# Attention sums of a macaron block: copied in two pieces, added and normalised on GpSimd into a resident buffer, with an output stage that loads nothing

## The reference

```python
x = x + 0.5 * ffn(layernorm(x), w_gate, w_up, w_down)
x = x + attn(layernorm(x), Wq, Wk, Wv, Wo, We)
x = x + 0.5 * ffn(layernorm(x), w_gate, w_up, w_down)

# attn
ctx = X @ We.T                                   # [1, 4096, 32]
influence = einsum('bqe,bke->bqk', ctx, ctx)
scores = einsum('bhqd,bhkd->bhqk', Q, K) * SCALE + 0.1 * influence[:, None]
out = einsum('bhqk,bhkd->bhqd', softmax(scores), V)
out = out.transpose(0, 2, 1, 3).reshape(b, s, d) @ Wo.T
```

## Time and profile before

| | us |
|---|---|
| median of 3 runs | 4047.24 (4041.54 to 4052.59) |
| the profiled execution | 4050.0 |
| its span | 4048.2 |
| attention's steps, 488 to 3695 | 3207 |
| output stage, 3695 to 3789 | 94 |
| second MLP, 3789 to the end | 259 |

### The profile page before, as it was taken

How to read it: one execution, slowest core, us unless ns; L and a number is a source line. 1 busy time by engine, 2 the same in 40 slices (tenths; PEclk the granted TensorE clock), 3 DMA queues, 4 the chain that set the end, 5 groups by cost and what they waited for, 6 DMA issues and landing times. The chain is left out here.

```text
span 4048.2 us, 91447 instructions
## 1 busy us (share of the span) xinstructions
PE 3807.0 (94%) x29204; PEld 2213.2 (55%) x29204; DVE 3249.4 (80%) x5168; ACT 2490.7 (62%) x2898; POOL 455.4 (11%) x274
## 2 busy tenths in 40 slices
PE   3998599999999999999999999999999999996698
PEld 2986355555555555555555555555555555553598
DVE  6984588878888888788888887888888878885697
ACT  4663266666666666666666666666666666663365
POOL 4980100000000000000000000000000000000397
PEclk7999699999999999999999999999999999997799
DMA  3004412121212121212121212121212121213200
GB/s 123 0 0 148 106 37 44 38 43 37 45 37 44 37 45 40 41 38 46 38 44 37 44 36 45 36 44 36 45 36 44 36 44 36 45 38 78 87 20 21
DMA packets 316697, 186.52 MB, mean 46 GB/s; under 512 B 195488, under 2 KB 246592, under 8 KB 315872
## 3 DMA queue, kind: packets, MB, share of 16 engines
q1 hardware_dynamic: 315248, 181.27, 20.5%
q10 hardware_dynamic: 1136, 1.08, 0.1%
HBM read 147.75 MB, written 33.82 MB: 45 GB/s over the span
## 5 line engine op out<-in xcount | busy, mean ns | idle before, releaser
L1185 DVE TENSOR_REDUCE tops<-coarse 128x1 f32<-128x512 f32 x4144 | 2681.2, 686 | 588.4 <-PE coarse L1046 484.6
L1161 ACT ACTIVATE probs<-fine 128x1024 f32<-128x1024 f32 x2048 | 1998.4, 1021 | 1018.2 <-PE fine L1065 1018.1
L1076 PE MATMUL o_ps<-probs,vh 128*32 128x512 f32 x8192 | 1092.3, 605 | 0.2 <-ACT probs L1161 0.2
L1055 PE MATMUL fine<-query_a,key_a 64*128 64x512 f32 x4096 | 922.7, 447 | 19.8 <-issue 19.1
L1055 PEld LDWEIGHTS fine<-query_a,key_a 64*128 64x128 f32 x4096 | 388.0, 186 | 929.4 <-ACT probs L1161 750.1
L1046 PE MATMUL coarse<-key_a,max_query 64*128 64x512 f32 x4144 | 834.4, 398 | 44.2 <-DMA key_c<-scratch_c_key 23.4
L1065 PE MATMUL fine<-query_b,key_b 33*128 33x512 f32 x4096 | 818.6, 395 | 0.0
L1061 PE MATMUL fine<-query_c,key_c 64*128 64x512 f32 x4096 | 816.3, 394 | 0.0
L1046 PEld LDWEIGHTS coarse<-key_a,max_query 64*128 64x128 f32 x4144 | 395.0, 187 | 114.5 <-DVE tops L1185 29.7
L1065 PEld LDWEIGHTS fine<-query_b,key_b 33*128 33x128 f32 x4096 | 389.2, 186 | 90.3
L1061 PEld LDWEIGHTS fine<-query_c,key_c 64*128 64x128 f32 x4096 | 389.4, 187 | 84.5
(11 more groups left out here) (157 smaller groups left out, 2326.0 us busy)
## 6 DMA issues: line engine op xcount, KB each, us to landing
query_c<-scratch_c_query SPq DMA_DIRECT2D x258, 128.0 KB, 2.7
max_query<-scratch_q_hi SPq DMA_DIRECT2D x524, 32.0 KB, 1.8
max_query<-scratch_c_query SPq DMA_DIRECT2D x262, 64.0 KB, 2.0
query_a<-scratch_q_hi SPq DMA_DIRECT2D x516, 32.0 KB, 1.8
query_a<-scratch_c_query SPq DMA_DIRECT2D x258, 64.0 KB, 2.0
query_b<-neg_max SPq DMA_DIRECT2D x1032, 0.5 KB, 2.0
query_b<-scratch_q_lo SPq DMA_DIRECT2D x258, 32.0 KB, 2.4
scratch_attended<-result SPq DMA_DIRECT2D x512, 8.0 KB
```

The costliest lines, as they stand in the source:

```text
L1055: pe.matmul(fine[i % 2][:, r, :], key_a[kp][half_rows(r, 0, HALF), cols], query_a[half][half_rows(r, 0, HALF), :], start=True, stop=False)
L1076: last = pe.matmul(o_ps[32 * j:32 * (j + 1), :], vh[kp][:, kt, :], probs[:, kt // 2 % RING, kt % 2, :], start=g == 0, stop=g == NG - 1)
L1161: act.activation(probs[:, i % RING, :, :], fine[i % 2][:, :, :], ACT.Exp).then_inc(probs_ready, 1)
L1185: dve.tensor_reduce(tops[n][:, idx // KB, idx % KB:idx % KB + 1], bank[:, :], AX.X, ALU.max).then_inc(tops_ready, 1)
```

## The change

**The sums of a step.** A class `Sums` holds the buffers. ScalarE copies `o_ps` in two pieces of 49 rows into two buffers, both starting at partition 0. GpSimd adds the two (`add_halves`), copies rows 32 to 48 of the sum down to row 0, and adds again (`add_quarters`): `total` has 16 rows of values and one of sums. SyncE copies the row of sums into `few`, 16 partitions of 32 elements; VectorE inverts it behind its eighth coarse reduction (`invert`); SyncE writes it to DRAM and reads it back spread over 16 rows into `wide`; GpSimd multiplies (`multiply`) one step later; and SyncE copies the product into `at`, which stays in SBUF for all 4096 tokens. `finish`, `take_result`, `sel` and the stores of values and sums are gone.

```diff
+    def add_halves(self, eng, s):
+        eng.wait_ge(self.ot_ready, s + 2)
+        eng.tensor_tensor(self.ot[0][:, :], self.ot[0][:, :], self.ot[1][:, :], ALU.add).then_inc(self.half_ready, 1)
+        eng.wait_ge(self.half_ready, s + 1)
+    def add_quarters(self, eng, s):
+        eng.tensor_copy(self.quarter[:, :], self.ot[0][32:32 + self.ROWS, :]).then_inc(self.quarter_ready, 1)
+        eng.wait_ge(self.quarter_ready, s + 1)
+        eng.tensor_tensor(self.total[:, :], self.ot[0][0:self.ROWS, :], self.quarter[:, :], ALU.add).then_inc(self.total_ready, 1)
+    def invert(self, eng, s):
+        eng.wait_ge(self.few_loaded, 16 * (s + 1))
+        eng.reciprocal(self.few[:, :], self.few[:, :]).then_inc(self.inv_ready, 1)
+    def multiply(self, eng, s):
+        eng.wait_ge(self.spread, 16 * (s + 1))
+        eng.tensor_tensor(self.wide[:, :], self.total[0:DK, :], self.wide[:, :], ALU.mult).then_inc(self.result_ready, 1)
...
+                def combine(s):
+                    sums.add_halves(pool, s)
+                    sums.multiply(pool, s - 1)
+                    sums.add_quarters(pool, s)
...
-                    act.wait_ge(fin_ready, F_LEAD + s)
-                    act.activation(ot[:, :], o_ps[:, :], ACT.Copy).then_inc(ot_ready, 1)
+                    act.wait_ge(sums.total_ready, s + 1)
+                    for half in range(2):
+                        last = act.activation(sums.ot[half][:, :], o_ps[2 * 32 * half:2 * 32 * half + 32 + sums.ROWS, :], ACT.Copy)
+                    last.then_inc(sums.ot_ready, 1)
```

```diff
+                def step(s, half, before_last, last):
+                    sp.wait_ge(probs_ready, P_LEAD + PAIRS * s)
+                    if within(s + 1):
+                        load_operand_a(1 - half, query_a, s + 1, q_loaded)
+                    if before_last is not None:
+                        sums.save_inverse(sp, s - 2)
...
+                        load_others(1 - half, s + 1)
+                    if before_last is not None:
+                        sums.spread_inverse(sp, s - 2)
+                        sp.wait_ge(sums.result_ready, s - 1)
+                    if last:
+                        sums.copy_sum(sp, s - 1)
...
+                        sums.store(sp, head, slice(block * QB, (block + 1) * QB) if isinstance(block, int) else bass.ds(block * QB, QB), sums.stored)
+                    if within(s + 1):
+                        load_max(s + 1, 1 - half)
+                    if within(s + 3):
+                        sp.wait_ge(coarse_ready, UNITS // 2 * (s + 2))
+                        load_operand_a(1 - half, max_query, s + 3, mq_loaded)
```

```diff
-                            if unit + 1 == FINISH_AFTER:
-                                before(lambda: finish(s - 1, UNITS * (s + 1) + FINISH_AFTER + 2 - COARSE))
...
+                        place = 2 if i % GROUP != 0 else 1 if unit == SKIP_AFTER + 1 else 0
+                        scores_first(s, half, kp, i)
+                        if place == 0:
+                            maxima(unit)
+                        scores_second(half, i)
+                        if place == 1:
+                            maxima(unit)
+                        scores_last(s, half, kp, i)
+                        if place == 2:
+                            maxima(unit)
```

```diff
+            with eng.Fori(0, H // 2 - 1) as hp:
+                two_heads(hp)
+            two_heads(H // 2 - 1)
...
+                for block in range(NQB - 2):
+                    step((H - 1) * NQB + block + 2, block % 2, (H - 1, block), True)
+                    for dst, src, loaded in reload[block:block + 1]:
+                        sp.dma_start(dst, src).then_inc(loaded, 16)
```

```diff
+                sp.wait_ge(sums.result_ready, LAST)
+                sums.store(sp, H - 1, tokens(NQB - 2), sums.late_stored)
+                for dst, src, loaded in more:
+                    sp.dma_start(dst, src).then_inc(loaded, 16)
+                sums.copy_sum(sp, LAST)
+                sums.save_inverse(sp, LAST)
...
+                def low(b, n):
+                    pool.wait_ge(ahi_ready, b + 1)
+                    if not isinstance(b, int) or b >= 2:
+                        pool.wait_ge(y_ready, b - 1)
+                    pool.tensor_tensor(at_lo[n][:, :, :], at[:, :, tokens(b)], at_hi[n][:, :, :].bitcast(F32), ALU.subtract).then_inc(alo_ready, 1)
```

```diff
+                    if has_next(b):
+                        x_norm(b + 1)
                     for i, (bank, scale, slot) in enumerate(SPLITS):
-                        if i == NEXT_AFTER - 1 and has_next(b):
-                            x_norm(b + 1)
                         if i == NEXT_AFTER and has_next(b):
                             x_lo(b + 1, 1 - n)
```

More of the change, by code:

```diff
@@ new lines, in _ @@
+                step(0, 0, None, False)
+                step(1, 1, None, True)
+                for block in range(2):
+                    step(block + 2, block, (0, block), True)
+                for head in range(H - 1):
+                    with sp.Fori(0 if head else 1, NQB // 2) as i:
+                        for half in range(2):
+                            block = 2 * i + half
+                            step(sp.snap(head * NQB + block + 2), half, (head, block), True)
+                    if head + 2 < H:
+                        load_keys_a(head % 2, head + 2)
+                        load_keys_b(head % 2, head + 2)
@@ new lines, in body @@
+                    if within(s + 2):
+                        reduce_max(s + 2, half, 0)
+                    if within(s + 1):
+                        max_rows(s + 1, 1 - half)
+                    if within(s + 2):
+                        for idx in range(1, INVERT_AFTER + 1):
+                            reduce_max(s + 2, half, idx)
+                    if unless_first is None:
+                        sums.invert(dve, s - 1)
+                    else:
+                        with dve.If(unless_first):
+                            sums.invert(dve, s - 1)
@@ L1359, in macaron_kernel @@
[L1359 to L1364 removed]
+        w_saved, o_reload, ffn_reload = sem("w_saved"), sem("o_reload"), sem("ffn_reload")
```

325 lines of the change are left out of this document (138 added, 187 removed).

## The result

The changed kernel takes **3952.97 us** (median of 4 runs, 3948.77 to 3958.01), the kernel before 4045.8 (4 runs, 4041.54 to 4052.59): a ratio of 0.977, with a 95% interval of 0.9751 to 0.9788. The forecast was 3945 and its range 3925 to 3980. The profiled execution took 3954.89 us, its span 3953.1, so the span is 95.1 us shorter than that of the profiled execution before.

A forecast was written before the change was run, and what follows sets the result against it. TensorE's own instructions were taken as the length of an attention step, VectorE next. Gains of 29 + 5 + 6 + 53 + 9 = 102 us from 4050 gave 3948, less 2.8 to the median 3945 us; range 3925 to 3980.

The forecast's parts named there:

- Part 1: Attention step: `finish` leaves TensorE, saving 0.27 us less a 0.04 wait in each of 127 steps; 29 us, ends 0 and 34.
- Part 2: ScalarE in attention: two copies of the sums instead of one, 598 ns each, nothing on the path.
- Part 3: GpSimd in attention: three two-input operations and a copy, 4.5 to 5.2 us a step, hidden; 0 us.
- Part 4: VectorE's inversion in attention: 0.3 us in idle time, `few` landed at 14.7, due at 18.8; costs nothing.
- Part 5: SyncE's chain ahead of `load_max` in an attention step: ends at 13.2, `load_max` began at 14.1; 0 us, ends 0 and +5.
- The rival with SyncE's chain (4072): Attention: chain DMAs land 2 to 3 us later, `load_max` some 6 late, TensorE waits about 1 us a step; 3%.
- Part 6: Attention's loop over two heads: six jumps back instead of seven, the last heads written out; gain 5 us, ends 0 and 5.5.
- Part 7: Last two attention steps: 24 pairs of coarse tiles beyond the end go, 0.25 us each; 6 us, ends 0 and 9.
- Part 8: Output stage, from attention's last product to the second MLP: 95 us becomes 42.5; gain 53, ends 43 and 55.
- Part 9: Projection: seven of TensorE's eight waits for the normalised block go; gain 9 us, ends 5 and 9.
- the one on the coarse wait: Attention: units 24 and 25 wait in their new place for what `finish` took, part 1 gives 0; 3974 us, 10%.
- GpSimd might block VectorE: Attention: VectorE stands still while GpSimd adds and becomes the bound, a step of 26.65 us; 4215 us, 4%.

The follow-up runs named there:

- experiment 1: The changed kernel with VectorE's reduction of coarse unit 24 reading 256 of its 512 columns: a step of 24.495 us instead of 24.622, a run of 3936.44 us.
- experiment 3: The kernel before without TensorE's adding products (`finish`), units 24 and 25 in the old place, then the new: steps 24.698 and 24.602 us, runs 4043.30 and 4024.10 us.
- Experiment 6: The changed kernel with three, then six more additions of 16x512 on GpSimd in each step: 4128.13 us and 4538.22 us.
- Experiment 5: The kernel before with only the last two heads written out and the projection's block normalised at the head: 4027.76 us, beside 4041.65 us for the kernel before.
- experiment 7: The changed kernel with, by version: all heads written out; all 128 steps, no skipped bank; also two low parts on VectorE: 3930.51, 3910.99, 3909.41 us.
- experiments 1 and 2: The second is the changed kernel with units 24 and 25 in the old place, behind their group's first product pair: a step of 24.710 us, a run of 3967.3.

## Why the prediction was right

**Part 1, `finish`: mis-sized.** Forecast 29 us, measured 16.2 in ordinary steps (0.137 each in place of 0.23). The step that failed is "a wait of 0 to 0.1 is left. I take 0.04". The prediction followed one wait, the one of the moved products (units 24 and 25), and that one costs nothing indeed. It did not follow the consequence of moving the products: their reductions come later by a pair, and the bank of unit 24 is the one that unit 27 wants. That wait takes 0.12 of the 0.26 us between the step before (24.76) and eight plain groups (24.50), where 0.04 were taken; experiment 1, in which it goes, has the step of eight plain groups. What was said of the old place was right: 24.70 to 24.71, nearly everything given back.

**Part 2, ScalarE: right.** 595 ns a copy. That nothing of it is on the path is contained in the 0.02 us of experiment 3.

**Part 3, GpSimd: right.** 1.28 + 1.27 + 0.60 + 1.28 = 4.4 us in a step (4.5 to 5.2 taken). With parts 2 and 5 it costs at most 0.02 us a step, by experiment 3.

**Part 4, the inversion: right** for this kernel. It takes 0.33 us, `few` is issued some 12 us into most steps (15 in the one behind a head's key loads, 11.6 in the one shown below), and VectorE waits for it three times: in the last two steps, where the coarse reductions ahead of it are missing, and in the output stage.

**Part 5, SyncE: the number right, the margin wrong.** `load_max` starts 14.0 us into the step, as reckoned:

```profile
3594.72 0.56 SPq L855 DMA_DIRECT2D few<-total  x1
3595.33 0.59 SPq L870 DMA_DIRECT2D at<-wide  x1
3597.11 5.03 SPq L1037 DMA_DIRECT2D query_b<-neg_max  x8
```

(The step begins at 3583.15; compare.) But "1 us before the chain is felt by SyncE, and some 4 more before TensorE feels it" is a margin of latency within one step. Experiment 6 shows another, the length of SyncE's own round: all but some 2 us of a step are issues, the work between them and waits for GpSimd, and that is the room there is on average; in the steps with key loads there is less. The rival with SyncE's chain (4072) put 1 us a step behind some 6 us of lateness of `load_max`; with three additions it is 4.6 us later on average, and 1.35 us a step are lost already.

**Part 6, the loop: right.** Forecast 5, measured 7.7, of which 5.1 for the seventh wrap and 2.6 because the six others are 0.4 us shorter on average. Of this, 0.14 for each of the seven belongs to part 1. They vary by 1.4 among themselves, so the rest isn't explained. Experiment 5 finds six wraps at 29.13 without the rest of the change, and experiment 7 shows the remaining six to be worth 28 us, of which its first version kept 23.

**Part 7, the tiles beyond the end: right.** Forecast 6, measured 5.5 in the last two steps. No run tests it alone.

**Part 8, the output stage: right.** Forecast 53, measured 95.1 - 40.1 = 55. The first product starts 6.2 us behind the start of attention's last one (6.4 taken), the first block's addition 5.5 later (5 taken), and the seven others follow in 23.9 us, 3.4 each (3.7 taken). They alternate between 2.9 and 4.2 us, and the chain of the last step can't be told from that. In the kernel before, the first addition came 41.0 us behind the start of attention's last product (now 11.7), and the seven others 7.1 to 8.1 us apart: some 29 us of the gain lie ahead of the first addition and 27 between the additions. From the last copy to the second MLP the nine kernels with the new stage take 37.3 to 39.0 us and the four with the old one 90.5 to 94.0, of which the kernel before is the longest (the one of experiment 5 takes 90.95). So some 3 us of the 55 can be scatter. No run takes the new stage apart further, but for the low parts in experiment 7.

**Part 9, the projection: a little small.** Forecast 9, measured 12.4 before attention's first copy, 11.0 in experiment 5. The first copy comes at 503.6 to 507.2 in the ten kernels with the new order and at 515.9 to 517.8 in the three with the old one, 11 us apart on average. The nine came from the row of TensorE's products, 15.3 to 6.2. The row of its weight loads, which wait first, went from 18.5 to 6.5, and these 12 us are the better measure.

**The second MLP**, forecast at 0, is 1.7 us longer. Its code is the same in all kernels of this study, and in the others, with the old or the new attention, it takes 260.7 to 264.1 us. So the 259.3 of the kernel before are the odd value, and this is no effect of the change.

In sum 29 + 5 + 6 + 53 + 9 = 102 stood against 16.2 + 7.7 + 5.5 + 55 + 12.4 - 1.7 = 95. Part 1 was 13 us too large, and parts 6, 8 and 9 were 8 us too small together, in part by scatter: that the total is off by only 7 is luck to that extent. The likeliest case held; of the rivals, the one on the coarse wait was half true, with a neighbour of the wait that it named. That GpSimd might block VectorE did not happen in attention, where the reductions stay at 686 ns, and did happen in the output stage, where it costs little.

## What to carry to other kernels

When instructions move in a ring of buffers, follow each buffer once round the ring: the wait that gets longer is not the one of the moved instruction, but of the next user of its buffer. When a chain is hidden behind a step, compare two things with the step: where the chain ends, and how long each queue on its way is occupied in one round, issues and waits together; the second was the tighter here (2 us against 5). Look also at the round that has most to do, and not at the mean alone. And an asymmetry that exists only so that a loop's body fits every round (the skipped bank) costs time in each step, which can be saved by writing the loop out: some 15 us of the 42 here; the other part is the loop's jumps.

## What was not expected of the hardware

An operation of VectorE with two inputs in SBUF stood still beside GpSimd's subtraction with two inputs in SBUF (2.83 us against 0.68), while 4096 reductions of VectorE out of PSUM kept their 686 ns beside GpSimd's additions and multiplications in every step. The Trainium skill (SBUF — State Buffer, SBUF: two separate sides) says that the two engines share a pair of ports which one of them holds for a whole instruction, on VectorE's side only for operations with two SBUF inputs or in a two-port mode; the rows agree with it in both directions. A second pair of rows of the changed kernel shows the same with the start 1.4 us later:

```profile
3668.21 2.42 POOL L1327 TENSOR_TENSOR o_at_lo<-at,o_at_hi 128x1024 fp32r<-128x1024 f32 x1 [0.63 <-ACT o_at_hi L1317]
3669.59 1.58 DVE L892 TENSOR_TENSOR wide<-total,wide 16x512 f32<-16x512 f32 x1 [0.20 <-DMA wide<-scratch_inv_sums]
```

Both times VectorE's operation ends 0.53 to 0.54 us behind the end of GpSimd's, whenever it began, and in experiments 1 and 2 and the first two versions of experiment 7 the addition takes 2.83 us as well. GpSimd pays too: its second low part, beside the end of the addition, took 2.83 us, the six behind it 2.38 to 2.42. So, as far as these rows go, what matters in moving work to GpSimd is what VectorE's own instructions read, and not how busy either is.

Writing out all 128 steps did not slow the engines: the step became the sum of its plain groups (24.50 us, eight of 3.06), and one jump of the long loop costs some 4.7 us (29.28 against 24.62).
